# Weighted values of an attention kernel: 256-column matmul pairs against 512-column matmuls, on one core

## The reference

```
q = layernorm(x) @ Wq.T + bq                       # 16 heads of 64
k = concat(side @ Wk.T + bk, ctx @ Wgk.T + bgk)    # 512 keys
v = concat(side @ Wv.T + bv, ctx @ Wgv.T + bgv)
p = softmax(where(mask, -inf, q k^T / 8))          # 256 x 512 a head
out = p @ v                                        # 256 x 64 a head
x = x + concat_heads(out) @ Wo.T + bo
x = x + ffn(layernorm(x))                          # fp8-quantised 256 x 256 product
```

## Time and profile before

| what | value |
|---|---|
| timed runs | 2606.21 and 2608.84 us, median 2607.53 us |
| span of the profiled execution | 2604.0 us |
| median of the timed runs less that span | 3.5 us |
| mean granted TensorE clock | 0.997 of full speed |
| one batch element in the loop | about 80.1 us |
| busy: TensorE, VectorE, GpSimd, ScalarE | 99%, 82%, 79%, 71% |

### The profile page before, as it was taken

One profiled execution on the slowest core, in us unless ns is written; L12 is line 12 of the kernel. 1 busy time (PEld: TensorE's weight loads), 2 busy tenths in 40 slices (PEclk: granted clock), 3 DMA queues, 4 the chain that ended last, 5 costly groups with the idle time before them and its releaser, 6 DMA issues.

```text
span 2604.0 us, 67670 instructions
## 1 busy us (share of the span) xinstructions
PE 2569.6 (99%) x20352; PEld 2356.3 (90%) x20352; DVE 2147.4 (82%) x5344; ACT 1856.5 (71%) x4464; POOL 2056.9 (79%) x2499
## 2 busy tenths in 40 slices
PE   7999999999999999999999999999999999999997
PEld 6899999999999999999999999999999999999996
DVE  7888888888878888888888888887888888888877
ACT  6776677777677766777677777767776677767775
POOL 6787777888778877778777788877887777877775
PEclk9999999999999999999999999999999999999999
DMA  5000000101000011000010000100000100001000
GB/s 159 17 24 25 32 24 24 32 16 32 28 28 24 16 32 32 24 24 24 24 32 25 25 31 16 32 28 28 24 16 32 32 24 24 29 19 32 28 17 13
DMA packets 59983, 75.19 MB, mean 29 GB/s; under 512 B 5168, under 2 KB 42032, under 8 KB 59952
## 3 DMA queue, kind: packets, MB, share of 16 engines
q1 hardware_dynamic: 59952, 74.81, 9.3%
HBM read 66.40 MB, written 8.39 MB: 29 GB/s over the span
## 4 chain that ended last, share of the span: by engine, by line
PE 97%; DVE 1%; ACT 0%; issue 0%; DMA 0%; SPq 0%; POOL 0%; POOLq 0%; DVEq 0%
PE ps_work L742 35%; PE ps_o L886 19%; PE ps_pt L870 18%; PE ps_work L858 15%; PE ps_work L819 8%; PE ps_work L828 1%; PE ps_work L798 1%; DVE probs L1518 0%; DMA wo_sb<-wgk_t_dram 0%; PE ps_work L824 0%; PE ps_work L787 0%; DVE pt_lo L1529 0%; DVE wgv_lo L1549 0%; ACT probs L1143 0%; SPq L387 0%
## 5 line engine op out<-in xcount | busy, mean ns | idle before, releaser
L549 POOL TENSOR_SCALAR probs<-probs,recips 128x512 f32<-128x512 f32 x1024 | 716.2, 711 | 198.0 <-DVE recips L1525 197.9
L1529 DVE TENSOR_TENSOR pt_lo<-ps_pt,pt_hi 128x512 fp32r<-128x512 f32 x1024 | 671.8, 682 | 159.1 <-ACT pt_hi L1150 154.1
L1143 ACT ACTIVATE probs<-probs,neg_max 128x512 f32<-128x512 f32 x1024 | 734.6, 722 | 63.0 <-DVE neg_max L1518 61.1
L1150 ACT CAST pt_hi<-ps_pt 128x512 fp32r<-128x512 f32 x1024 | 560.7, 591 | 301.3 <-PE ps_pt L870 290.0
L1518 DVE CUSTOM_DVE_ANT_1 probs<-ps_work,mask_sb 128x512 f32<-128x512 f32 x960 | 618.8, 683 | 69.4 <-PE ps_work L858 66.3
L870 PE MATMUL ps_pt<-ident,probs 128*128 128x128 f32 x4096 | 557.8, 275 | 3.4 <-DVE pt_lo L1529 1.9
L886 PE MATMUL ps_o<-pt_hi,v_hl 128*128 128x256 f32 x2048 | 537.7, 296 | 0.1
L870 PEld LDWEIGHTS ps_pt<-ident,probs 128*128 128x128 f32 x4096 | 455.8, 141 | 71.5 <-issue 52.0
L886 PE MATMUL ps_o<-pt_lo,v_hl 128*128 128x256 f32 x2048 | 508.3, 281 | 0.0
L886 PEld LDWEIGHTS ps_o<-pt_hi,v_hl 128*128 128x128 f32 x2048 | 386.8, 189 | 34.9 <-issue 34.5
L886 PEld LDWEIGHTS ps_o<-pt_lo,v_hl 128*128 128x128 f32 x2048 | 388.5, 190 | 0.1
(11 more groups left out here) (125 smaller groups left out, 5921.7 us busy)
## 6 DMA issues: line engine op xcount, KB each, us to landing
mask_sb<-mask_dram SPq DMA_DIRECT2D x128, 256.0 KB, 3.4
x_sb<-x_dram SPq DMA_DIRECT2D x32, 256.0 KB, 2.7
side_raw<-side_t_dram SPq DMA_DIRECT2D x32, 256.0 KB, 3.7
scr_b<-ctx_t_dram SPq DMA_DIRECT2D x32, 256.0 KB, 2.7
out_dram<-y SPq DMA_DIRECT2D x31, 256.0 KB, 2.1
wo_sb<-wo_t_dram SPq DMA_DIRECT2D x1, 1024.0 KB, 5.5
v_bias<-bv_dram SPq DMA_DIRECT2D x1, 512.0 KB, 6.6
v_bias<-bgv_dram SPq DMA_DIRECT2D x1, 512.0 KB, 7.8
```

The source lines that it names most:

```text
L549: nc.gpsimd.tensor_scalar(p, p, recips[:, h % RING, t:t + 1], 1.0, ALU.mult, ALU.mult).then_inc(norm_done, 1)
L1143: nc.scalar.activation(p, p, ACT.Exp, bias=neg_max[:, h % RING, t:t + 1], scale=-1.0, accum_out=sums[:, h % RING, t:t + 1]).then_inc(exp_d ...
L1150: nc.scalar.copy(pt_hi[:, h % 2, 2 * k:2 * k + 2, :], ps_pt[:, k, :, :]).then_inc(pthi_done, 1)
L1529: V.tensor_tensor(pt_lo[:, h % 2, 2 * k:2 * k + 2, :], ps_pt[:, k, :, :], pt_hi[:, h % 2, 2 * k:2 * k + 2, :].bitcast(F32), ALU.subtract). ...
```

## The change

`pt_hi` and `pt_lo` become two views of one tensor in which the halves lie side by side for each key tile. `outputs` then issues one matmul of 512 columns per key tile in place of two of 256, into the whole bank of `ps_o`: columns 0 to 255 collect the product with `pt_hi`, columns 256 to 511 that with `pt_lo`. `o_los` is as it was, so it takes v_lo·pt_hi; v_lo·pt_lo is not added any more. `o_adds` becomes two additions with a wait between them.

```diff
-        pt_hi = sb("pt_hi", [P, 2, KT, S], F32R)
-        pt_lo = sb("pt_lo", [P, 2, KT, S], F32R)
+        pt_split = sb("pt_split", [P, 2, KT, 2, S], F32R)
+        pt_hi, pt_lo = (pt_split[:, :, :, i, :] for i in range(2))
...
+        o_part = sb("o_part", [DK, S], F32)
...
+        o_part_done = sem("o_part_done")
...
                     if kt % 2 == 0:
                         pe.wait_ge(ptlo_done, 2 * c.head(h) + kt // 2 + 1)
-                    for pt in (pt_hi, pt_lo):
-                        last = mm(ps_o[:, h % 2, 0:S], v_hl[:, n % 2, kt, i, :], pt[:, h % 2, kt, :],
-                                  start=(kt == 0 and pt is pt_hi), stop=(kt == KT - 1 and pt is pt_lo))
+                    last = mm(ps_o[:, h % 2, :], v_hl[:, n % 2, kt, i, :],
+                              pt_split[:, h % 2, kt, :, :].rearrange("p a s -> p (a s)"),
+                              start=(kt == 0), stop=(kt == KT - 1))
                 last.then_inc(o_full, 1)
...
                     dst = o_first[:] if h == 0 else o_t[e * DK:(e + 1) * DK, pair, :]
-                    V.tensor_tensor(dst, ps_o[0:DK, e, 0:S], o_lo[:], ALU.add).then_inc(o_done, 1)
+                    V.tensor_tensor(o_part[:], ps_o[0:DK, e, S:2 * S], o_lo[:], ALU.add).then_inc(o_part_done, 1)
+                    dve.wait_ge(o_part_done, c.head(h) + 1)
+                    V.tensor_tensor(dst, ps_o[0:DK, e, 0:S], o_part[:], ALU.add).then_inc(o_done, 1)
```

## The result

The changed kernel takes 2682.24 us (2681.3 and 2683.19) against 2607.53 us: a ratio of 1.0284 (95% interval 1.0254 to 1.0314), so 2.8% slower. The forecast was 2688 us.

What follows compares the result with a forecast made beforehand. TensorE was taken to bound the kernel. Stalls of 3.3 us less 0.8 for faster matmuls gave 2.5 us a batch element, +80 us over 32: 2684 us on the span, 2688 us timed; own range 2655 to 2725.

Steps and rivals of the forecast that it cites:

- What bounds the kernel: Whole kernel: TensorE, busy 99% of the span, so each nanosecond taken from its stream shows if the others keep up.
- The signs: Profile after: VectorE near 90% busy, TensorE 95 to 97%, a batch element of 82.6 us.
- The wide matmul: Outputs, L886: one 512-column matmul for two of 256 saves 0.0125 us a pair, 26 us in all (10 to 44).
- The added time: Second addition in VectorE's stream: 0.34 to 0.45 us a head, taken as 0.45, or 7.2 us a batch element.
- The first four places of the walk: TensorE starts at 1024.35, 1037.56, 1049.05 and 1062.25: stalls of 0.50, 1.0, 0.6 and 0.45 us behind late VectorE.
- the walk: One batch element followed start by start: stalls of 3.3 us less 0.8 for faster matmuls, net 2.5 us.
- D: VectorE's lag against the times of before: plus 0.45 us at each addition, reduced when VectorE waits for TensorE or ScalarE.
- D at 1037.56: Chunk after the minimum of head 10: four additions pile VectorE's lag up to 1.45 us, 0.24 us to spare.
- The fifth place: Transposes at 1068.23: late `recip` delays GpSimd's pair, then TensorE; a stall of 0.7 us, 0.28 us to spare.
- rival 1: VectorE's idle time and waits absorb the lag; only the gain stands, 2582 us, up to about 2655; chance 0.31.
- rival 2: VectorE paces everything: all 7.2 us a batch element come through, less 0.8, giving 2812 us; chance 0.05.
- rival 3: Wide matmul much cheaper, weight load setting its step (some 131 ns by the skill); 2525 us; chance 0.04.

Runs made afterwards that it cites:

- the run with the small addition: Three chained additions a head in the changed kernel, the middle one cut to one column, output complete: 2975.79 us (1.1419).

## Why the prediction was right, point by point

- *What bounds the kernel.* Right: TensorE, until VectorE is late. The signs were somewhat off: VectorE is busy 86% where near 90 was expected, TensorE 98% where 95 to 97 was. The run with one addition shows that time taken from TensorE comes out in full (11 us).
- *The wide matmul.* The direction was right, the size at the range's lower end. Four matmuls take 1.08 us with the last one's own 0.39, so three steps of 0.23 us, where 0.225 was taken: 11 us gained instead of 26. L858, the row of the same type, was the better neighbour, and the middle between the two rows was a guess.
- *The added time.* Right: 0.43 to 0.45 us from addition to addition. What 0.34 would give back was mis-sized: the bounds had 19 us, from five places, and the run without the wait shows 45.
- *The first four places of the walk.* Each showed, with the releaser named there: GpSimd's norm at the first, a minimum at the second, the addition at the next two. The spares were read rightly (at the outputs of head 10, a D of 1.63 less the 0.62 that were to spare is the 1.01 measured); the lags D that reached them were too large, 2.3 having been forecast there. The term that was most mis-sized is D at 1037.56: 1.45 us was forecast, which left a step of 1.0. The line of 1037.11, with which that minimum ends, is the one below in the changed kernel, and 1067.56 - 29.57 - 1037.11 is a D of 0.88; the step was 0.49:

```profile
1067.56 0.08 DVE L1520 DVE_READ_ACCUMULATOR2_ANT neg_max<- 128x1 f32 x1
```

Four additions did pile up, but 0.32 us of it went at once in a quantising step that stands between the first and the second of them. It took 1.20 us before and took 0.88 here, and the reason can be read beside GpSimd's lines (VectorE's step of the changed kernel; GpSimd's instruction of the changed kernel, then the same one of before):

```profile
1051.24 0.88 DVE L1402 TENSOR_TENSOR scr_a<-scr_a,scr_b 128x512 f32<-128x512 f32 x1
...
1049.97 1.59 POOL L544 TENSOR_TENSOR v_hl<-kv_out,v_hl 128x512 fp32r<-128x512 f32 x1
...
1020.05 1.80 POOL L542 TENSOR_TENSOR v_hl<-kv_out,v_hl 128x512 fp32r<-128x512 f32 x1
```

The step ends 0.55 us after GpSimd's instruction in both kernels (1022.40 after 1021.85, 1052.12 after 1051.56), however early it starts, and so it does in 31 rounds of each trace. It acts as a wait for GpSimd, which the profile doesn't list as one, and such a wait sets D back to GpSimd's lag of 0.14 us. The prediction's waits were those for TensorE and ScalarE alone. The remaining 0.25 us are small gaps that took more than the 0.45 given to them, and a start from 0.03 instead of 0.1. GpSimd's own lag shrank in the same way before the first place, from 0.36 to 0.15 us, which made that step 0.24 instead of 0.50. In the whole run the two quantising steps that got shorter went from a mean of 1188 ns to 870 and from 932 to 618, as the groups of the changed kernel show:

```profile
L1402 DVE TENSOR_TENSOR scr_a<-scr_a,scr_b 128x512 f32<-128x512 f32 x32 | 27.8, 870 | 1.0
...
L1398 DVE TENSOR_SCALAR scr_b<-scr_b 128x512 f32<-128x512 f32 x32 | 19.8, 618 | 1.0
```

- *The fifth place.* The loss was there, 0.51 us where 0.7 was forecast, but not by the path that was named. It was to come through `recip` and GpSimd's norm, at the transposes. In fact 0.42 of it comes one action earlier, at the scores of 1098.73 above, which wait for a minimum of VectorE directly; only 0.09 are left at the transposes.
- *What was not in the walk.* It ended at 1068.23. Two more losses came behind: the chunk behind the minima of the next element (0.25 us), and `wo0_prev`, which started late behind ScalarE's copy of keys (0.33 us; the row of L821 above, 30 times 0.5 us for its weight load). ScalarE was late because its exponentials had waited 1.87 us for minima, and these stand behind additions in VectorE's list:

```profile
1101.64 0.72 ACT L1145 ACTIVATE probs<-probs,neg_max 128x512 f32<-128x512 f32 x1 [1.87 <-DVE neg_max L1520]
...
1105.79 0.51 PEld L821 LDWEIGHTS ps_work<-wo_sb,o_t 128*128 128x128 f32 x3 [0.52 <-ACT kv_out L1122]
```

Together 0.58 us. The three errors, too small a gain, too large a pile and a missed end, cancelled: 2.38 us a batch element against 2.5. So the mechanism was right and the closeness of the total, 6 us, was in part luck.
- *The rivals.* The lag is not absorbed (rival 1), though two thirds of the added 7.2 us a batch element are. VectorE doesn't pace everything (rival 2) at 0.45 us; at 0.90 us a head, some 60 to 77% of the further time passes through. The wide matmul has no step of 0.13 us (rival 3).

## What to carry to other kernels

A busy share of 82% says nothing of whether the engine can take more: read, for each start of the bounding engine, how long before it its releaser ended. Here some eight places in 80 us, with between nothing and 0.6 us to spare, made 2.8% out of work that fitted as a sum, and moving additions away from them took most of it back. A gain from fewer and wider matmuls is small when the type streams no faster: measure the step on the nearest row of the same type. And look for instructions whose length depends on when they start: such a one hides a wait for another engine, and it swallows lag like any other wait.

## What the runs showed of the hardware that was not expected

**A short VectorE addition that isn't short.** The one-column addition reads both operands from SBUF. Its durations run from 150 ns to 1155 (the tiles it writes, with least, median and most ns):

```profile
L1545 DVE TENSOR_TENSOR o_small<-o_spare x512: 150/358/1155, 46.4 to 2952.6; 64x1 f32<-64x1 f32 x171
```

and the quantising steps, which also work in SBUF alone, changed theirs by 0.3 us when the schedule shifted, while the additions of 256 columns that read PSUM kept within 381 and 421 ns. GpSimd is busy 69% of this run's time. The trace shows what the long ones have in common: all 257 that took over 200 ns start while a GpSimd instruction runs, and all of them end within 50 ns of the end of one. An example, VectorE's line and then GpSimd's, with ends at 1008.66 and 1008.65:

```profile
1007.57 1.09 DVE L1545 TENSOR_TENSOR o_small<-o_spare 64x1 f32<-64x1 f32 x1
...
1007.37 1.28 POOL L546 TENSOR_TENSOR v_hl<-kv_out,v_hl 128x512 fp32r<-128x512 f32 x1
```

Of the 255 short ones, 161 start while no GpSimd instruction runs and 94 in the last 0.1 us of one. The Trainium skill (page "SBUF — State Buffer", section "SBUF: two separate sides") says that a VectorE operation with two SBUF inputs and a GpSimd operation that reads SBUF share a pair of ports by an exclusive lock, held for a whole instruction. By that rule the small addition would take its 150 ns alone and wait for the end of a GpSimd instruction otherwise, and the quantising step with two SBUF inputs would end a fixed time after GpSimd's. The ends above agree; no run took GpSimd away to show it.

**Code loading at a loop's head.** Nearly 3 us in 29 of the rounds, once there are 16 more VectorE instructions a round. TensorE then stands too, for 3.25 us in the round shown below, and behind that its granted clock is at the lower level (1.2 GHz) for some 3 us, as the steps of 0.213 us show. The run's mean granted clock falls from 0.997 to 0.983 of full speed, and to 0.967 in the run with the small addition. VectorE's timeline of the run with three additions:

```profile
1021.04 0.69 DVE L1521 CUSTOM_DVE_ANT_1 probs<-ps_work,mask_sb 128x512 f32<-128x512 f32 x1 [3.22 <-issue]
```

and TensorE's, in the same round:

```profile
1021.79 0.39 PE L745 MATMUL ps_work<-kv_hi,wk_hi 128*128 128x256 f32 x1 [3.25 <-DVE neg_max L1521]
```

The Trainium skill (page "Runtime: NRT & Kernel Launch", section "Instruction fetch mechanics") says that a taken branch to code outside the two blocks that an engine holds makes it wait for a transfer. The 29 waits, one at each jump back, agree; the changed kernel itself has none of them.
